# Routing tokens to experts: one product for gate and transpose, variance on all partitions, batches of 3, 3, 3, 2, 1

## What is computed

```python
h = (t - mean(t)) / sqrt(var(t) + 1e-5)            # _ln_t, over the 256 channels
logits = h @ gate_w + gate_b                       # [4608, 8]
probs = softmax(logits)
idx = argmax(probs); prb = probs[idx]
pos = cumsum(one_hot(idx))[idx] - 1                # place in the expert's queue
kept = pos < 720                                   # capacity
buf[idx, pos] = h                                  # for the kept tokens
y = (relu(buf @ w1 + b1) @ w2 + b2)[idx, pos] * prb * kept
t = t + y
```

## Time and profile before

| | us |
|---|---|
| three executions: lowest, median, highest | 5525.89, 5541.01, 5549.51 |
| the profiled execution | 5545.61 |
| its span, first to last instruction | 5543.8 |
| routing stage in it, 4982.6 to 5150.3 | 167.7 |

### The profile page before, as it was taken

The page is one execution under the profiler, slowest core; times in us unless marked ns, Lnnn a source line. Parts: engine busy times, 40 slices in busy tenths (PEclk is TensorE's granted clock), DMA queues, the critical chain, the costliest instruction groups (busy, mean ns, idle before and its releaser), DMA issues. The chain is left out here.

```text
span 5543.8 us, 51619 instructions
## 1 busy us (share of the span) xinstructions
PE 4723.3 (85%) x14958; PEld 2624.9 (47%) x14959; DVE 3434.4 (62%) x5148; ACT 2126.5 (38%) x3464; POOL 2317.8 (42%) x2114
## 2 busy tenths in 40 slices
PE   5787788988878888799899899596999899996798
PEld 3333333433323333355455655464555555555576
DVE  2999999999999999679387365264232101003232
ACT  2666666656656666232232222111222222112232
POOL 2888898888889888302111100461000000003111
PEclk7999999999999999999999899798999999995899
DMA  2434443443444443100100001110112000001222
GB/s 85 153 111 145 141 124 123 131 128 117 131 141 130 130 136 109 61 31 6 50 30 15 31 4 42 22 16 15 58 43 89 2 0 2 0 8 36 64 73 93
DMA packets 222219, 391.88 MB, mean 71 GB/s; under 512 B 35986, under 2 KB 205752, under 8 KB 217116
## 3 DMA queue, kind: packets, MB, share of 16 engines
q1 hardware_dynamic: 213852, 383.83, 21.6%
q0 software_dynamic: 8128, 5.27, 0.6%
HBM read 337.13 MB, written 58.23 MB: 71 GB/s over the span
## 5 line engine op out<-in xcount | busy, mean ns | idle before, releaser
L934 POOL TENSOR_TENSOR DBU<-DU,BB 128x461 f32<-128x461 f32 (+1 forms) x1280 | 1372.3, 1087 | 291.7 <-DVE PS L978 279.3
L624 PE MATMUL PS<-G,ident 128*128 128x461 f32 (+1 forms) x2560 | 1138.1, 570 | 385.2 <-DVE G L989 382.5
L978 DVE TENSOR_TENSOR_SCAN PS<-PS,HC,DBU 128x461 f32<-128x461 f32 (+1 forms) x1024 | 1149.5, 1168 | 3.9 <-ACT PS L796 2.5
L796 ACT ACTIVATE PS<-DT,alog 128x461 f32<-128x461 f32 (+1 forms) x1280 | 825.1, 645 | 727.5 <-DVE PS L978 726.7
L624 PEld LDWEIGHTS PS<-G,ident 128*128 128x128 f32 x2560 | 451.9, 190 | 1034.8 <-DVE G L989 822.7
L989 DVE TENSOR_TENSOR G<-PS,CB 128x461 f32<-128x461 f32 (+1 forms) x1280 | 786.6, 625 | 3.4 <-PE PS L624 3.4
L3074 DVE TENSOR_TENSOR X<-X,PS 128x768 f32 x12 | 11.5, 954 | 554.0 <-PE PS L3041 554.0
L3030 PE MATMUL PS<-QT,N 128*128 x864 | 310.1, 486 | 5.5 <-ACTq L3047 5.5
L3041 PE MATMUL PS<-AT,XT 128*128 128x384 f32 x864 | 310.4, 487 | 0.0
L1367 POOL TENSOR_TENSOR X<-X,FF x12 | 42.5, 3542 | 636.7 <-ACT EV L1362 636.7
L978 DVE TENSOR_TENSOR_SCAN PS<-PS,DBU 128x461 f32<-128x461 f32 (+1 forms) x256 | 271.7, 1106 | 57.8 <-POOL DBU L934 55.7
(11 more groups left out here) (446 smaller groups left out, 7459.0 us busy)
## 6 DMA issues: line engine op xcount, KB each, us to landing
BB<-proj_dram SPq DMA_DIRECT2D x256, 461.0 KB, 4.0
CB<-proj_dram SPq DMA_DIRECT2D x64, 922.0 KB, 6.0
BB<-proj_dram SPq DMA_DIRECT2D x64, 460.0 KB, 4.7
ew<-in_l_w SPq DMA_DIRECT2D x16, 1024.0 KB, 5.7
CB<-proj_dram SPq DMA_DIRECT2D x16, 920.0 KB, 5.9
w_fc<-in_l_w_fc SPq DMA_DIRECT2D x4, 2048.0 KB, 11.7
XI<-xi_dram SPq DMA_DIRECT2D x8, 928.0 KB, 5.0
xi_dram<-XI SPq DMA_DIRECT2D x8, 922.0 KB, 6.5
```

Of the source, the lines that this page charges most:

```text
L624: pe.matmul(PS[:, j, :wide(g)], k.ident[:], G[:, S % 4, :wide(g)], start=False, stop=(n == DS - 1))\
L796: act.activation(DA(S), DT[:, j, :wide(g)], ACT.Exp, scale=w.alog[:, chunk(g)[1], j, n:n + 1]).then_inc(da_done, 1)
L934: pool.tensor_tensor(DBU[:, S % 4, :wide(g)], DU[:, j, :wide(g)], BB[:, 2 * u + n % 2, :wide(g)], ALU.mult).then_inc(dbu_done, 1)
L978: dve.tensor_tensor_scan(flow(HS(S), g), flow(DA(S), g), flow(DBU[:, S % 4, :wide(g)], g), start, ALU.mult, ALU.add).then_inc(h_done, 1)
```

## The change

Four edits in `route_images`, nothing elsewhere.

1. The identity (128 columns) and the gate weights (8) stand side by side in `turn_w`. One f32 product per tile and channel half gives the transposed tile and this half's part of the logits, 136 columns. ScalarE copies the 2 x 8 raw logits into `RAW` and the 256 channels into `XT`, and VectorE adds the two halves in `shift`. The separate gate products go.
2. The variance is one product of `mean_w` [128, 128] with the squares, 384 columns, so that every partition holds it. ScalarE computes exp(-0.5 ln(var + eps)) on [128, 384]. The root, the reciprocal and the spread products go.
3. The table set with logarithm and exponential is loaded once at the head of ScalarE's program.
4. Batches of 3, 3, 3, 2 and 1 pieces instead of 3, 3, 3, 3. Shift, choose and place of a batch run 4, 5 and 6 steps after its last piece, all behind the multiplication.

```diff
+    BATCH = (3, 3, 3, 2, 1)
+    SCATTER = BATCH[0] + 6
...
 # gpsimd
-                    if s >= 2 * QV + 3:
+                    if s >= SCATTER:
...
 # tensor
-                        for t in range(TT):
-                            mm = pe.matmul(k.PS[:, 2 + v % 2, t:t + 1], sq[:, v % DEEP, 0, t * P:(t + 1) * P],
-                                           k.mean_w[:, 0:1], start=True, stop=True)
-                        mm.then_inc(var_ready, 1)
+                        pe.matmul(k.PS[:, 2 + v % 2, :T], k.mean_w[:], sq[:, v % DEEP, 0, :], start=True, stop=True)\
+                          .then_inc(var_ready, 1)
...
-                                mm = pe.transpose(k.PS[:, 4 + n % 2, i * P:(i + 1) * P], k.N[:, i, at:at + P], k.ident[:])
+                                mm = pe.matmul(k.PS[:, 4 + n % 2, i * WIDE:(i + 1) * WIDE], k.N[:, i, at:at + P],
+                                               turn_w[:, i, :], start=True, stop=True)
                             mm.then_inc(t_ready, 1)
-                        for t in range(TT):
-                            at, lg = (v % NT) * T + t * P, (r * TT + t) * NE
-                            for i in range(KC):
-                                mm = pe.matmul(k.PS[:, 6 + q % 2, lg:lg + NE], k.N[:, i, at:at + P], gate_w[:, i, :],
-                                               start=(i == 0), stop=(i == KC - 1))
-                        mm.then_inc(lg_ready, 1)
-                    if 2 <= s <= NV + 1:
-                        v = s - 2
-                        pe.wait_ge(inverted, v + 1)
-                        for t in range(TT):
-                            mm = pe.matmul(k.PS[:, 2 + v % 2, P + t * P:2 * P + t * P],
-                                           rstd[:, v % DEEP, t:t + 1].broadcast_to([P, P]), k.ident[:],
-                                           start=True, stop=True)
-                        mm.then_inc(spread, 1)
...
 # scalar
+                act.preload_act_table_set("natural_log_exp_and_others")
...
-                        act.activation(rstd[:, v % DEEP, :], k.PS[:, 2 + v % 2, 0:TT], ACT.Sqrt, bias=k.eps5[:])\
-                           .then_inc(rooted, 1)
+                        act.activation(rstd[:, v % DEEP, :], k.PS[:, 2 + v % 2, :T], ACT.Ln, bias=k.eps5[:]).then_inc(logged, 1)
+                        act.drain()
+                        act.activation(rstd[:, v % DEEP, :], rstd[:, v % DEEP, :], ACT.Exp, scale=-0.5).then_inc(inverted, 1)
...
-                            act.activation(XT[:, n, 0:C], k.PS[:, 4 + n % 2, 0:C], ACT.Copy).then_inc(t_done, 1)
+                            turned = k.PS[:, 4 + n % 2, 0:KC * WIDE].rearrange("p (i c) -> p i c", i=KC)
+                            act.activation(RAW[:, n, :, :], turned[:, :, P:WIDE], ACT.Copy)
+                            act.activation(XT[:, n, 0:C].rearrange("p (i c) -> p i c", i=KC), turned[:, :, 0:P], ACT.Copy)\
+                               .then_inc(t_done, 1)
...
 # vector
-                    if s >= 2 * QV and s % QV == 0:
-                        shift(s // QV - 2)
...
-                    if 1 <= s <= NV:
-                        v = s - 1
-                        dve.wait_ge(rooted, v + 1)
-                        dve.reciprocal(rstd[:, v % DEEP, :], rstd[:, v % DEEP, :]).then_inc(inverted, 1)
...
-                        dve.wait_ge(spread, v + 1)
-                        root = k.PS[:, 2 + v % 2, P:P + T].rearrange("p (o t) -> p o t", o=1).broadcast_to([P, KC, T])
+                        dve.wait_ge(inverted, v + 1)
+                        root = rstd[:, v % DEEP, :].rearrange("p (o t) -> p o t", o=1).broadcast_to([P, KC, T])
...
+                    for q in batch_at(s, 6):
+                        place(q)
+                    for q in batch_at(s, 5):
+                        choose(q)
+                    for q in batch_at(s, 4):
+                        shift(q)
```

More of the change, by code:

```diff
@@ L3229, in route_images, with last, width, slots @@
     NV = NB * NT
-    QV = 3
-    QT_ = QV * TT
-    NQ = NV // QV
+    BATCH = (3, 3, 3, 2, 1)
+    NQ = len(BATCH)
+    QT_ = max(BATCH) * TT
+    WIDE = P + NE
+    SCATTER = BATCH[0] + 6
+    def last(q):
+        return sum(BATCH[:q + 1]) - 1
+    def width(q):
+        return BATCH[q] * TT
+    def slots(q):
+        return slice((last(q) + 1 - BATCH[q]) * TT, (last(q) + 1) * TT)
+    def batch_at(s, lag):
+        return [q for q in range(NQ) if last(q) + lag == s]
     with ExitStack() as ctx:
@@ L3261, in ring, with each, every @@
             return slice(v % NT * T, (v % NT + 1) * T)
[L3263 to L3267, removed]
+        def each(ap, q):
+            return ap.rearrange("p (t o) -> p t o", o=1).broadcast_to([P, width(q), NE])
+        def every(ap, q):
+            return ap.rearrange("p (o e) -> p o e", o=1).broadcast_to([P, width(q), NE])
         with nc.Block() as block:
@@ L3282, in scatter @@
                 def scatter(t):
[L3283 to L3287, removed]
+                    for q in range(NQ):
+                        if t == slots(q).start:
+                            pool.wait_ge(slot_done, q + 1)
+                            pool.wait_ge(t_done, slots(q).stop)
+                    if t == 0:
+                        pool.wait_ge(k.buf_clear, 16 * (ZN + ZY))
                     pool.indirect_dma_start(
@@ L3304, in _ @@
                             .then_inc(sq_summed, 1)
-                    if s >= 2 * QV + 3:
+                    if s >= SCATTER:
                         for t in range(TT):
-                            scatter(TT * (s - 2 * QV - 3) + t)
-                for t in range(TT * (NV + 2 - 2 * QV - 3), TM):
+                            scatter(TT * (s - SCATTER) + t)
+                for t in range(TT * (NV + 2 - SCATTER), TM):
                     scatter(t)
@@ L3391, in _ @@
                             act.wait_ge(t_ready, n + 1)
-                            act.activation(XT[:, n, 0:C], k.PS[:, 4 + n % 2, 0:C], ACT.Copy).then_inc(t_done, 1)
-                    if s >= 2 * QV and s % QV == 0:
-                        exp(s // QV - 2)
-                exp(NQ - 1)
+                            turned = k.PS[:, 4 + n % 2, 0:KC * WIDE].rearrange("p (i c) -> p i c", i=KC)
[3 more added lines that the diff above has]
+                    for q in batch_at(s, 4):
+                        exp(q)
+                for q in range(NQ):
+                    if last(q) + 4 >= NV + 3:
+                        exp(q)
             @block.vector
@@ L3401, in shift @@
                 def shift(q):
-                    dve.wait_ge(lg_ready, QV * (q + 1))
-                    logits = k.PS[:, 6 + q % 2, 0:QT_ * NE].rearrange("p (t e) -> p t e", e=NE)
-                    dve.tensor_tensor(LG[:], logits, every(gate_b[:]), ALU.add)
+                    lg, w = LG[:, 0:width(q), :], slice(0, width(q))
+                    dve.wait_ge(t_done, slots(q).stop)
+                    dve.tensor_tensor(lg, RAW[:, slots(q), 0, :], RAW[:, slots(q), 1, :], ALU.add)
                     dve.drain()
-                    dve.tensor_reduce(mx, LG[:], AX.X, ALU.max)
+                    dve.tensor_tensor(lg, lg, every(gate_b[:], q), ALU.add)
@@ L3454, in place @@
                     dve.drain()
-                    dve.tensor_tensor(kept, kept, pos, ALU.add)
+                    dve.tensor_tensor(kp, kp, ps_, ALU.add)
                     dve.drain()
-                    dve.tensor_tensor(SI[:, at], kept, base, ALU.add).then_inc(slot_done, 1)
+                    dve.tensor_tensor(SI[:, slots(q)], kp, bs, ALU.add).then_inc(slot_done, 1)
                 dve.memset(PF[:, 0, :], 0.0)
                 dve.memset(ones[:], 1.0)
+                for i in range(KC):
+                    mm = dve.tensor_copy(turn_w[:, i, 0:P], k.ident[:])
@@ L3461, in _ @@
+                mm.then_inc(turn_set, 1)
                 dve.wait_ge(tok_in, 16)
```

106 lines of the change are left out of this document (57 added, 49 removed).

## The result

The changed kernel took 5501.62 us (median of 6 runs, 5476.89 to 5505.92) beside 5542.32 us of the kernel before (6 runs, 5525.89 to 5552.86): ratio 0.9922, 95% interval 0.9904 to 0.9941, 40.7 us faster. The profiled execution of after took 5505.92 us, its span 5504.2.

What follows compares the result with a forecast made beforehand. Waits in the routing stage, not one engine's sum, were taken as the bound. Gains of 24 + 17.5 + 11 - 0.5 = 52 us gave 5493.6 from the profiled execution, 5489.0 from the median; range 5471 to 5509.

Steps and rivals of the forecast that it cites:

- What bounds: Routing stage, 168 us of the 5543.8 us span: waits bound it, not one engine's sum.
- the loop: Plain step from mean product through ScalarE's chain to third tile: 6.0 us at the lower clock, 4.8 upper, against 8.16.
- First slots: Stage start to the first batch's slots: 20.6 us earlier at the lower clock, 25.8 at the upper; 24 taken.
- First distance: First to second batch's slots, 40.7 us before: gain 16.6 at the lower clock, 19.5 at the upper; 17.5 taken.
- Second distance: Second to third batch's slots, 27.1 us before: gain 9.9 at the lower clock, 12 at the upper; 11 taken.
- Batches: Batches of 3, 3, 3, 2, 1: gain nothing, cost nothing; four batches would end at the same time.
- The spare: Time by which the fourth and fifth batches' slots are ready before their scatters are due: 2.7 and 1.6 us.
- Contention (d): GpSimd slowed beside VectorE's SBUF work: 0.5 us taken, at most 11.4; as a rival 53 us slower, 5594, chance 0.03.
- (b): ScalarE's logarithm and exponential in two table sets, two loads each loop: loop 8.6 us, gain 24, time 5517; chance 0.05.
- (c): Weight load and stream in series in TensorE's new tile products: 2.56 us more a step, gain about 24, 5517; chance 0.05.
- a ring: GpSimd's squares are queued behind scatters that wait for VectorE's slots; TensorE's next variance product comes 9.79 us after its last work.
- the batch chain: A batch's path from last logits to slots: 8.46 us before, 8.8 forecast; over 9 if the last scatters show gaps.

Runs made afterwards that it cites:

- the third experiment: Changed kernel with batches of 3, 3, 3, 3 in place of 3, 3, 3, 2, 1: 5477.46 us, ratio 0.989.
- the last session: One session: changed kernel again 5494.84 us; scatters one step later 5468.36; that with batches of 3, 3, 3, 3 5473.26; kernel before 5532.56.
- later scatters: Changed kernel with GpSimd's scatters begun one step later (SCATTER = BATCH[0] + 7): 5478.4 us, ratio 0.9889; timed again 5468.36 us, ratio 0.9891.

## Why the prediction was right, and where not

**What bounds, and the loop.** Right. The step came out at 4.72 us for a forecast of 4.8 (upper clock) or 6.0 (lower). The run with a second logarithm shows that ScalarE's work stands on it, the one with more products that TensorE's doesn't.

**First slots.** Forecast 24, measured 27.3. The mechanism is the forecast's; the size is that of its other end, 25.8 at the upper clock and a bit beyond. I had weighed the lower clock in; the stage's plain steps had 0.99. I had no row that could tell beforehand which level would be granted.

**First distance.** Forecast gain 17.5, measured 14.8: a term that was mis-sized. Part of it is the 0.5 us for contention, which failed in its direction: I priced only what VectorE does to GpSimd. One more small thing is on the path: the second batch's `choose` operations, which run beside GpSimd's scatters. They took 3.95 us (5053.87 to 5057.82) in after. In the changed kernel run again they met GpSimd at other moments:

```profile
5054.30 0.22 DVE L3426 TENSOR_REDUCE red<-LG 128x9 f32<-128x72 f32 x1
...
5055.80 0.23 DVE L3437 TENSOR_TENSOR POS<-OH,key 128x72 f32<-128x72 f32 x1
...
5056.41 0.23 DVE L3441 TENSOR_TENSOR OH<-POS,red 128x72 f32<-128x72 f32 x1
```

2.34 us, with each at 0.23; the clock in the scatters ahead of them was 0.72 instead of 0.62, and that distance was 22.8 us, gain 17.9. These operations make up 1.6 of the 3.1 us between the two executions; what made the rest isn't separated. So the term isn't a number but 15 to 18 us, and the forecast lies in it.

**Second distance.** Forecast 11, measured 9.8 (and 9.9 again), which is the forecast's lower-clock figure of 9.9.

**Batches.** Right: nothing, by the third experiment and again by the last session. The spare was named as 2.7 and 1.6 us. It was larger: the last batch's slots came 7.6 us after the fourth's, not 8.8, and stood at 101.9 us of the stage while their scatters were due at 106.3; with about 0.9 us from slots to scatter that leaves 3.5. Even so it was used up four times: see the last section.

**Contention (d).** Forecast 0.5 in a range of 0 to 11. By the run with the root in PSUM the multiplication's second SBUF operand costs less than two executions of one text differ (2.1 us). The Trainium skill (GPSIMD Engine Reference, Key points) says that GpSimd contends for its SBUF interfaces with VectorE instructions of two SBUF inputs. The trace agrees in kind: the first scatter took 1.91 us beside such a multiplication and 1.20 with the root in PSUM. The trace shows further that VectorE's instruction is held as well, 1.77 against 0.23.

**Rivals (b) and (c).** Neither came: one table load, and tile products 0.12 us apart at the upper clock. (b) is now priced by a run instead of by argument, at 24.6 us of gain (26.4 without the pauses of the last section) where I had 24. My 5 us for its first slots didn't follow from its loop: four loops of 2.6 us more leave 10 of the 20.6. The run had 6.5 (63.9 against 70.4), in steps of 8.6 us.

**The total.** 5489.0 forecast, 5501.62 measured; the stage's gain was hit at 51.6 for 52, and the sum still missed by 12.6 us. That the stage came within 0.4 us is partly luck: the first slots gave 3.3 us more than I took, the two distances 2.7 and 1.2 less, and the same text had a stage of 114.0 us the second time, a gain of 53.7. The unnamed step is the first one: "the sum is made against the profiled execution" takes for granted that the other 5376 us stay. They moved by 12 us in the profile, with no change to them, in a range of 38 us between executions (4957.9 to 4996.3). The six us that I added to the range at each end for the scatter of a median are too few for that; the range held because the stage's bounds were generous.

## What to carry to other kernels

Write the loop of a step out link by link, with each engine's in-order queue, before pricing an edit: the gain of the removed products was set by ScalarE's chain, which no removed instruction belonged to. Where a shared in-order queue closes a ring (here GpSimd's squares behind its scatters), moving one item by a step, a change of one digit, was worth 8 to 11 us of the stage, about the second distance's whole gain. And cut the span at fixed instructions before comparing: the stage says what the edit did to within a microsecond or two, while the same text's medians lie 10 us apart and its single executions up to 38 (5457.91 and 5496.35).

## What the runs showed of the hardware that I had not expected

**One loop, two lengths.** 38.5 or 61.3 us for the same twelve steps, by the granted clock in them (0.87 and 0.96 against 0.50 from 3480 to 3500 us), in one and the same program. In the long form TensorE was busy without a break and yet stayed at the lower level; I can't say from these traces what decides it.

**Operations held.** A VectorE operation of 72 elements, 0.23 us everywhere in before, took 1.77 us beside GpSimd's instructions in after, others of its kind 0.94 and 0.68, and GpSimd's first scatter took 1.91 instead of 1.20. It isn't small operations alone: a multiplication of 0.95 us took 1.74 in after, 2.66 with later scatters and 3.22 without the preload, and never more than 0.95 with its root in PSUM. Running at the same time doesn't suffice: with the second logarithm the multiplication started 0.11 us behind the first scatter instead of 0.11 ahead of it, and they took 0.95 and 1.20.

**Gaps without a releaser.** In all four kernels of the second session (no preload, root in PSUM, second logarithm, more products) VectorE paused up to 1.9 us between small operations of the last batch, with nothing that it waited for. From the run with the root in PSUM, GpSimd and VectorE, the last batch:

```profile
5088.06 0.17 DVE L3457 COPY PF<-PF 128x8 f32<-128x8 f32 x1 [1.20 <-issue]
...
5090.87 0.17 DVE L3462 TENSOR_SCALAR red<-red 128x3 f32<-128x3 f32 x1 [1.90 <-issue]
...
5093.70 0.16 DVE L3469 TENSOR_TENSOR red<-red 128x3 f32<-128x3 f32 x1 [1.85 <-issue]
...
5094.88 0.97 POOL L3305 DMA_INDIRECT buf_dram<-XT,SI  x1 [2.09 <-issue]
```

That batch's slots came 13.0 us after the fourth batch's (94.0 to 107.0) instead of 7.6. These 5.4 us used up the spare of 3.5, and the scatters got a gap of 2.09 us instead of 0.30: 1.8 us for the stage. "If the last scatters show gaps, the batch chain is longer than 9 us", said the prediction; here it was longer by pauses, not by work. No profile of the other sessions shows such pauses of over 0.5 us in VectorE; their cause is open. With later scatters the spare is wider, since 27 scatters stand in one row: the last batch's slots were there at 88.8 us of the stage and due at 95.7, and with four batches at 81.5 and due at 87.7.
